# Keys of the last four groups turned by transfer from DRAM, a shorter warm-up, and two late scalings moved to VectorE

## The chip, the cores and the metric

The kernel runs on one core of a Trainium2 chip. The metric is the device time of one execution in microseconds (us). The engines of a core run side by side, each through its own list in order: TensorE (PE, its weight loads PEld), VectorE (DVE), ScalarE (ACT), GpSimd (POOL) and SyncE (SP), which here only issues transfers. They meet in semaphores. All numbers are fp32.

## What is computed

Two cross-attention layers over 128 batch items of 64 tokens (width 128). The first attends with the layer-normed tokens to two key sources (`a` and `v`) of 64 rows of width 64 each, then adds a dense layer with a residual. The second attends to the first source alone.

```
q = _ln(x1, g1, b1) @ Wq + bq;  k = _ln(x2, g2, b2) @ Wk + bk;  v = _ln(x2, g2, b2) @ Wv + bv
attn = softmax(einsum('bqe,bke->bqk', q, k) * scale);  ctx = attn @ v;  cma = ctx @ Wo + bo
output = cma_a(x, ctx_512) + cma_v(x, fside) + x
x = _ln(output, ln_g, ln_b) @ fc_W + fc_b + output
Q, K, V = x @ Wq + bq, ctx_512 @ Wk + bk, ctx_512 @ Wv + bv
out = x + softmax(Q K^T * scale) V @ Wo + bo
```

## The kernel before

Weights are folded once at the start (`fold_*` on PE, `copy_*` on ACT and DVE), so that Wq and Wk become one matrix `m0`. The rest is 16 groups of 8 batch items, all in tiles of 128 partitions x 512. One group passes on PE through: `t0` (queries times m0), `cfT` (keys transposed), `s0` (scores), `prob0T`, `mix0`, `out0`, `resN`, `dense`, `x1T`, then the second layer `t1`, `s1`, `prob1T`, `mix1`, `out1`. Between two of these steps another engine empties the PSUM bank: ACT copies and exponentials (`softmax0`, `softmax1`), four ACT scalings per group in `gain` behind `dense`, DVE statistics, maxima, sums and residuals, POOL the products that need no PSUM: `scale_cf` and `shift_cf` (layer norm of the keys), `scale_xt` (layer norm of queries that came already transposed), `probs0` and `probs1` (division by the softmax sum).

The order is written out by hand, engine by engine, as a list of calls; each call waits on semaphores for its inputs and for the buffer that it overwrites. A call that waits holds up all that stands behind it on its engine.

Three places matter here.

- **The ramp.** PE begins with `keep_busy`, multiplications of a constant (`ident` by `ones`) whose result nobody reads: 13, later 3, 1 and 1, eighteen in all. One such call is two matmul records in the trace.
- **The keys.** A group's keys come as `cf_sb` (key rows on partitions). DVE takes their statistics, ACT makes the reciprocal deviation, POOL `scale_cf` makes `cfv_sb` (also the values of `mix0`) and `shift_cf` makes `cfk_sb`, PE `cfT` transposes it with four 128x128 multiplications and ACT `copy_cfT` brings it to `cfT_sb`, which `s0` reads.
- **The spread of the scalings.** For groups 4 to 15 the queries come transposed, so that a token's scaling must lie along the free axis on every partition. PE `turn_rows(b)` transposes the 40 rows of scalings of a batch (two groups; batches 7 and 8 are groups 12, 13 and 14, 15), ACT `copy_rowsT` copies them, SP `store_rows` writes 20 KB to DRAM, SP `spread_x` reads it back to all 128 partitions (512 KB), POOL `scale_xt` multiplies. The code for the same with keys (`load_kt`, `spread_k`, `spread_s`, `scale_kt`, `shift_kt`) is there but not used, since `KEY_BATCHES` is empty.

Outputs leave through three slots of `out_sb` (`final` on DVE, `store` on SP).

Of the kernel before, what the change touches and what calls it, by code (L numbers as in the profile page):

```python
# [8 lines left out]
ALU = mybir.AluOpType  # L9
# [19 lines left out]
KEY_BATCHES = []  # L29
# [5 lines left out]
GAIN_ON_DVE = []  # L35
# [31 lines left out]
def attention_kernel(nc, x, xt, cf, kt, ct, wq, wk, wv, w128, wt, cols128, rows_dram, out):  # L67
    with ExitStack() as ctx:
# [3 lines left out]
        def sem(name):  # L72
# [76 lines left out]
        rsum1 = sb("rsum1", [P, GROUPS, PAIRS])  # L149
# [57 lines left out]
        exp1_bias_done, exp1_done, rsum1_done, prob1_done, final_done = (  # L207
            sem(s) for s in ("exp1_bias_done", "exp1_done", "rsum1_done", "prob1_done", "final_done"))
# [110 lines left out]
        def _(sp):  # L319
# [108 lines left out]
            load_x(11)
            store_rows(4)
            load_x(12)  # L430
            load_ct(4)
            load_x(13)
            load_xt(6)
            spread_x(4)
            load_ct(5)
            load_xt(7)
            load_cf(9)
            load_xt(8)
            load_xt(9)
            store_rows(5)  # L440
            load_x(14)
            load_cf(10)
            load_x(15)
            spread_x(5)
            load_cf(11)
            load_ct(6)
            store(0)
            store(1)
            load_xt(10)
            load_ct(7)  # L450
            load_ct(8)
            load_xt(11)
            load_xt(12)
            load_cf(12)
            store_rows(6)
            spread_x(6)
            load_cf(13)
            load_xt(13)
            store(2)
            load_ct(9)  # L460
# [12 lines left out]
            load_ct(13)
            spread_x(8)
            store(5)
            store(6)
            store(7)
            load_ct(14)
            load_ct(15)
# [12 lines left out]
        def _(pool):  # L492
# [89 lines left out]
            def probs1(g):  # L582
# [51 lines left out]
            scale_xt(8)
            probs1(3)
# [1477 lines left out]
```

## Time and profile before

| | |
|---|---|
| median of 3 runs | 154.44 us (153.74 to 155.4) |
| the profiled execution, its own time | 154.15 us |
| its span (first to last instruction) | 152.1 us |
| busy: PE, PEld, DVE | 144.1 (95%), 104.1 (68%), 119.7 (79%) us |
| busy: ACT, POOL | 117.0 (77%), 83.7 (55%) us |
| chain that ended last, by engine | PE 92%, ACT 3%, issue 2%, DVE 1% |
| moved by DMA | 23.40 MB, mean 154 GB/s |

The span is 2.05 us less than that execution's time; the rest lies outside the span. "Issue" is time in which an engine waited for nothing that the profile shows. A PE record's duration includes the drain of the array and overlaps the next, so what a block of PE work takes from the engine is read from its start to the next block's start.

### The profile page before, as it was taken

The numbers are of one execution on the slowest core, as the hardware profiler recorded it, in microseconds if no ns is written. First come the engines' busy times: TensorE is split into PE (matmuls) and PEld (weight loads), VectorE is DVE, ScalarE is ACT, GpSimd is POOL, SyncE is SP. The second block draws the span as 40 slices with busy tenths as digits, with TensorE's granted clock in tenths as the row PEclk, the third lists the DMA queues.
The fourth block names the chain that finished last, engine by engine and source line by source line (L and its number), as shares of the span: only waits on it lengthen the run. The fifth ranks groups of instructions, "written<-read, shape, count | busy, mean of one in ns | idle before, by whom it ended". The sixth has DMA issues, their size and how long they took to land.

```text
span 152.1 us, 6148 instructions
## 1 busy us (share of the span) xinstructions
PE 144.1 (95%) x2320; PEld 104.1 (68%) x2320; DVE 119.7 (79%) x351; ACT 117.0 (77%) x410; POOL 83.7 (55%) x112
## 2 busy tenths in 40 slices
PE   5999999799999999999999999999999999999771
PEld 5987767688566766656866767657874877766440
DVE  1557999968899979899889757988677799668733
ACT  3436778568989788967977999787996878796970
POOL 2566999679438861878177575595674141201220
PEclk9999999999999999999999999999999999999998
DMA  5995799570770608786445019707300402201215
GB/s 154 346 386 179 227 312 370 142 274 3 238 241 15 211 8 263 237 232 186 165 144 173 4 43 244 248 8 249 135 4 0 142 2 73 73 0 69 75 71 207
DMA packets 13449, 23.40 MB, mean 154 GB/s; under 512 B 1660, under 2 KB 4332, under 8 KB 13420
## 3 DMA queue, kind: packets, MB, share of 16 engines
q1 hardware_dynamic: 12988, 22.61, 45.6%
q8 instruction: 18, 0.29, 0.8%
q10 hardware_dynamic: 432, 0.41, 0.8%
q14 instruction: 11, 0.09, 0.2%
HBM read 18.69 MB, written 4.32 MB: 151 GB/s over the span
## 4 chain that ended last, share of the span: by engine, by line
PE 92%; ACT 3%; issue 2%; DVE 1%; POOL 0%; POOLq 0%; ACTq 0%
PE ps L1758 10%; PE ps L1740 10%; PE ps L1699 9%; PE ps L1773 6%; PE ps L1731 6%; PE ps L1709 6%; PE ps L1747 6%; PE ps L1766 5%; PE ps L1574 5%; PE ps L1808 5%; PE ps L1684 5%; PE ps L1719 5%; PE ps L1783 4%; PE ps L1800 3%; PE ps L1791 2%
## 5 line engine op out<-in xcount | busy, mean ns | idle before, releaser
L579 POOL TENSOR_TENSOR prob<-exp,rsum 128x512 f32<-128x512 f32 x16 | 16.7, 1044 | 23.6 <-DVE rsum L1231 23.4
L585 POOL TENSOR_TENSOR prob<-exp,rsum 128x256 f32<-128x256 f32 x16 | 9.8, 616 | 19.7 <-DVE rsum L1300 19.6
L539 POOL TENSOR_TENSOR cfv_sb<-cf_sb,rows 128x512 f32<-128x512 f32 x16 | 17.0, 1061 | 5.8 <-PE ps L1731 3.5
L844 ACT ACTIVATE exp<-ps,exp_bias 128x64 f32<-128x64 f32 x64 | 19.3, 322 | 1.0 <-DVE exp_bias L1295 0.9
L825 ACT ACTIVATE gain_sb<-ps,res_rstd 128x128 f32<-128x128 f32 x64 | 18.3, 372 | 1.6 <-PE ps L1758 1.2
L547 POOL TENSOR_TENSOR cfk_sb<-cfv_sb,rows 128x512 f32<-128x512 f32 x16 | 17.0, 1060 | 1.1 <-POOL rows L532 0.2
L1758 PEld LDWEIGHTS ps<-wd,resT_sb 128*128 128x128 f32 x128 | 15.8, 191 | 2.3 <-issue 1.9
L1758 PE MATMUL ps<-wd,resT_sb 128*128 128x130 f32 x128 | 17.3, 278 | 0.0
L1699 PE MATMUL ps<-zT_sb,m 128*128 128x512 f32 x32 | 17.0, 617 | 0.0
L1740 PE MATMUL ps<-mix_sb,w 128*128 128x512 f32 x32 | 16.8, 608 | 0.0
L555 POOL TENSOR_TENSOR zT_sb<-xt_sb,x_spread 128x512 f32<-128x512 f32 x12 | 15.2, 1278 | 2.7 <-DMA x_spread<-rows_dram 2.4
L1241 DVE SCALAR_TENSOR_TENSOR resT_sb<-ps,out_bias,xt_sb 128x512 f32<-128x512 f32 x16 | 12.0, 748 | 4.6 <-PE ps L1740 4.4
L1186 DVE BATCH_NORM_STATS2 cf_stats<-cf_sb 128x6 f32<-128x128 f32 x64 | 13.8, 281 | 1.1 <-DMA cf_sb<-in_cf 1.1
L844 ACT ACTIVATION_READ_ACCUMULATOR exp<-ps,exp_bias 128x1 f32 x64 | 13.7, 214 | 0.0
L1278 DVE SCALAR_TENSOR_TENSOR x1T_sb<-ps,row_bias,resT_sb 128x512 f32<-128x512 f32 x16 | 11.9, 741 | 2.2 <-PE ps L1766 1.9
L1308 DVE TENSOR_TENSOR out_sb<-ps,x1T_sb 128x512 f32<-128x512 f32 x16 | 11.0, 687 | 3.3 <-PE ps L1808 3.1
L1247 DVE BATCH_NORM_STATS2 res_stats<-ps 128x6 f32<-128x256 f32 x32 | 12.0, 417 | 1.8 <-PE ps L1747 1.7
L1227 DVE TENSOR_REDUCE sum<-exp 128x8 f32<-128x512 f32 x16 | 10.8, 678 | 3.0 <-ACT exp L802 2.9
L815 ACT COPY mix_sb<-ps 128x512 f32<-128x512 f32 x16 | 9.5, 592 | 4.5 <-PE ps L1731 4.5
L1216 DVE TENSOR_REDUCE max<-ps 128x8 f32<-128x512 f32 x16 | 10.9, 680 | 2.3 <-PE ps L1709 2.3
L789 ACT ACTIVATE t_sb<-ps,m 128x512 f32<-128x512 f32 x16 | 11.0, 689 | 2.1 <-PE ps L1699 2.0
L1179 DVE BATCH_NORM_STATS2 x_stats<-x_sb 128x6 f32<-128x256 f32 x32 | 11.9, 414 | 0.0
(148 smaller groups left out, 342.5 us busy)
## 6 DMA issues: line engine op xcount, KB each, us to landing
x_sb<-in_x SPq DMA_DIRECT2D x16, 256.0 KB, 3.8
xt_sb<-in_xt SPq DMA_DIRECT2D x16, 256.0 KB, 3.9
out<-out_sb SPq DMA_DIRECT2D x16, 256.0 KB, 2.2
cf_sb<-in_cf SPq DMA_DIRECT2D x15, 256.0 KB, 3.3
x_spread<-rows_dram SPq DMA_DIRECT2D x6, 512.0 KB, 4.7
ct_sb<-in_ct SPq DMA_DIRECT2D x16, 128.0 KB, 4.0
w_sb<-in_w SPq DMA_DIRECT2D x1, 448.0 KB, 4.5
cf_sb<-in_cf ACTq DMA_DIRECT2D x1, 256.0 KB, 4.5
```

Of the source, the lines that this page charges most:

```text
L539: pool.tensor_tensor(cfv_sb[:, g % CFV_SLOTS, :, :, :], cf_sb[:, g % CF_SLOTS, :, :, :], wide_cf(cf_rstd, g), ALU.mult).then_inc(cfv_pool, 1)
L547: pool.tensor_tensor(cfk_sb[:, at % CFK_SLOTS, :, :, :], cfv_sb[:, g % CFV_SLOTS, :, :, :], wide_cf(cf_shift, g), ALU.add).then_inc(cfk_po ...
L555: pool.tensor_tensor(zT_sb[:, g % ZT_SLOTS, :], xt_sb[:, g % XT_SLOTS, :], x_spread[:, slot, half, :], ALU.mult).then_inc(zT_scaled, 1)
L579: pool.tensor_tensor(prob0[:, g % PROB0_SLOTS, :, :, :], exp0[:, g % EXP0_SLOTS, :, :, :], wide0(rsum0, g), ALU.mult).then_inc(prob0_done, 1)
L825: last = nc.scalar.mul(gain_sb[:, g % GAIN_SLOTS, p, :], ps[:, bank + p // 2, at:at + D], res_rstd[:, g, p // 2, p % 2:p % 2 + 1])
L844: last = nc.scalar.activation(exp1[:, g % EXP1_SLOTS, p, :], ps[:, bank + u, v * S:(v + 1) * S], ACT.Exp, bias=exp1_bias[:, g, p:p + 1], a ...
L1186: last = v.bn_stats(cf_stats[:, g, p, :, :].rearrange("p h k -> p (h k)"), cf_sb[:, g % CF_SLOTS, p, :, :].rearrange("p h c -> p c h"))
L1241: v.scalar_tensor_tensor(resT_sb[:, g % REST_SLOTS, :], ps[:, bank, :], out0_bias[:, 0:1], xt_sb[:, g % XT_SLOTS, :], ALU.add, ALU.add).th ...
L1247: last = v.bn_stats(res_stats[:, g, u, :, :].rearrange("p v k -> p (v k)"), ps[:, bank, 2 * u * P:2 * (u + 1) * P].rearrange("p (v d) -> p ...
L1699: mm(ps[:, bank, :], m0[:, 0:2 * C], zT_sb[:, g % ZT_SLOTS, :], start=True, stop=True).then_inc(t0_made, 1)
L1740: mm(ps[:, bank, :], w01[:, 0:D], mix0_sb[:, g % MIX0_SLOTS, :, :, :, :], start=True, stop=True).then_inc(out0_made, 1)
L1758: last = mm(ps[:, bank + p // 2, at:at + D + 2], resT_sb[:, g % REST_SLOTS, p * P:(p + 1) * P], wd[:, 0:D + 2], start=True, stop=True)
```

## The change

1. `KEY_BATCHES = [7, 8]`: for groups 12 to 15 the keys are loaded a second time, already transposed (`load_kt`, 256 KB each). Their scalings and shifts are spread by `spread_k` and `spread_s` (two transfers of 256 KB each, four per batch). POOL `scale_kt` multiplies and `shift_kt` adds, straight into `cfT_sb`. `shift_cf`, `cfT` and `copy_cfT` of these groups are gone; `scale_cf` stays for the values.
2. Ten `keep_busy` multiplications instead of eighteen: 8 at the start and two single ones later. The folds stand in another order (`fold_wv` first), and so do the first loads.
3. `GAIN_ON_DVE = [14, 15]`: one DVE multiplication of 128x512 from PSUM (`early_gain`) in place of four ACT scalings, for the last two groups.
4. `PROB1_ON_DVE = [15]`: `probs1(15)` is made by DVE (`late_probs1`) instead of POOL, with a semaphore of its own.
5. The order of calls and the PSUM banks are new on every engine, from the first call to the last.

```diff
-KEY_BATCHES = []
+KEY_BATCHES = [7, 8]
-GAIN_ON_DVE = []
+GAIN_ON_DVE = [14, 15]
+PROB1_ON_DVE = [15]
...
+            def late_probs1(g):
+                dve.wait_ge(rsum1_done, g + 1)
+                need(dve, prob1T_made, g - PROB1_SLOTS + 1)
+                v.tensor_tensor(prob1[:, g % PROB1_SLOTS, :, :], exp1[:, g % EXP1_SLOTS, :, :],
+                                wide1(rsum1, g), ALU.mult).then_inc(prob1_dve, 1)
...
-            keep_busy(13, 0)
-            fold_v(0)
-            fold_a(6)
-            keep_busy(3, 2)
+            keep_busy(8, 0)
+            fold_wv(0)
+            fold_v(1)
+            fold_a(3)
```

The loaded keys' code, which was there before:

```
def spread_k(b):
    ...
    for h in range(2):
        sp.dma_start(k_spread[HALF[h], ...], rows_dram[at, 8 + 16 * h:16 + 16 * h, :]....broadcast_to([C, 8 * P]))
def scale_kt(g):
    pool.tensor_tensor(blocks(ks_sb[...]), kt_sb[...], blocks(k_spread[:, slot, half, :]), ALU.mult)
def shift_kt(g):
    pool.tensor_tensor(cfT_sb[...], blocks(ks_sb[...]), blocks(s_spread[:, slot, half, :]), ALU.add)
```

**The order on PE at the start.** Before, the first eleven rows after the entry (`ones,ident` is `keep_busy`, `wq_sb` and `wk_sb` the folds of the query and key weights, `z_sb` is `zT(0)`, `cols_sb,w_sb` `fold_bias`, `wkT_a,wqT_a` the first row of `fold_m0`):

```order
L1574 MATMUL ps<-ones,ident 128x128 x13
L1577 MATMUL ps<-affine_v,wq_sb 128x129
L1578 MATMUL ps<-affine_v,wk_sb 128x64
L1577 MATMUL ps<-affine_a,wq_sb 128x129
L1578 MATMUL ps<-affine_a,wk_sb 128x64
L1574 MATMUL ps<-ones,ident 128x128 x3
L1677 MATMUL ps<-ident,z_sb 128x128 x4
L1625 MATMUL ps<-cols_sb,w_sb 128x1
L1626 MATMUL ps<-cols_sb,w_sb 128x1
L1574 MATMUL ps<-ones,ident 128x128
L1604 MATMUL ps<-wkT_a,wqT_a 128x64
```

And of the change, in the same place (`wt_sb,w_sb` is the second row of `fold_am`, `affine_a,wv_sb` is `fold_wv`):

```order
L1592 MATMUL ps<-ones,ident 128x128 x8
L1635 MATMUL ps<-affine_a,wv_sb 128x65
L1635 MATMUL ps<-affine_v,wv_sb 128x65
L1595 MATMUL ps<-affine_v,wq_sb 128x129
L1596 MATMUL ps<-affine_v,wk_sb 128x64
L1595 MATMUL ps<-affine_a,wq_sb 128x129
L1596 MATMUL ps<-affine_a,wk_sb 128x64
L1643 MATMUL ps<-cols_sb,w_sb 128x1
L1644 MATMUL ps<-cols_sb,w_sb 128x1
L1664 MATMUL ps<-cols_sb,w_sb 128x1
L1665 MATMUL ps<-wt_sb,w_sb 128x64
L1622 MATMUL ps<-wkT_a,wqT_a 128x64
```

`zT(0)` now stands behind `fold_m0`, and `fold_wv` and `fold_am` ahead of it; four `keep_busy` between the folds are gone.

**The order on POOL in the last third.** Before, from `probs0(12)` on (`exp,rsum 128x512` is `probs0`, 128x256 `probs1`, `xt_sb,x_spread` is `scale_xt(14)` and `(15)`, `cfk_sb` is `shift_cf`):

```order
L579 TENSOR_TENSOR prob<-exp,rsum 128x512
L555 TENSOR_TENSOR zT_sb<-xt_sb,x_spread 128x512 x2
L585 TENSOR_TENSOR prob<-exp,rsum 128x256
L539 TENSOR_TENSOR cfv_sb<-cf_sb,rows 128x512
L579 TENSOR_TENSOR prob<-exp,rsum 128x512
L547 TENSOR_TENSOR cfk_sb<-cfv_sb,rows 128x512
L579 TENSOR_TENSOR prob<-exp,rsum 128x512
L585 TENSOR_TENSOR prob<-exp,rsum 128x256
```

And of the change, again from `probs0(12)` on (`ks_sb<-kt_sb,k_spread` is `scale_kt`, `cfT_sb<-ks_sb,s_spread` is `shift_kt`):

```order
L591 TENSOR_TENSOR prob<-exp,rsum 128x512
L567 TENSOR_TENSOR zT_sb<-xt_sb,x_spread 128x512 x2
L576 TENSOR_TENSOR ks_sb<-kt_sb,k_spread 128x512
L585 TENSOR_TENSOR cfT_sb<-ks_sb,s_spread 128x512
L576 TENSOR_TENSOR ks_sb<-kt_sb,k_spread 128x512
L597 TENSOR_TENSOR prob<-exp,rsum 128x256
L591 TENSOR_TENSOR prob<-exp,rsum 128x512
L585 TENSOR_TENSOR cfT_sb<-ks_sb,s_spread 128x512
L591 TENSOR_TENSOR prob<-exp,rsum 128x512
L597 TENSOR_TENSOR prob<-exp,rsum 128x256
```

Three key operations stand between `scale_xt(15)` and `probs1(9)` (the first row of 128x256), where none stood.

**The order on SP around the rows of batch 7.** Before (`rows_dram<-rowsT` is `store_rows(7)`, then `load_cf(14)`, `load_ct(10)`, `spread_x(7)`, `load_ct(11)`, `load_cf(15)`):

```order
L346 DMA rows_dram<-rowsT 40x128
L332 DMA cf_sb<-in_cf 128x512
L341 DMA ct_sb<-in_ct 128x256
L353 DMA x_spread<-rows_dram 128x1024
L341 DMA ct_sb<-in_ct 128x256
L332 DMA cf_sb<-in_cf 128x512
```

And of the change (`out<-out_sb` is `store(3)`, later `store(4)`; `cf_sb<-in_cf` is `load_cf(14)`, later `load_cf(15)`; the first `ct_sb` is `load_ct(12)`):

```order
L350 DMA rows_dram<-rowsT 40x128
L395 DMA out<-out_sb 128x512
L336 DMA cf_sb<-in_cf 128x512
L345 DMA ct_sb<-in_ct 128x256
L357 DMA x_spread<-rows_dram 128x1024
L367 DMA k_spread<-rows_dram 64x1024 x2
L395 DMA out<-out_sb 128x512
L336 DMA cf_sb<-in_cf 128x512
L377 DMA s_spread<-rows_dram 64x1024 x2
```

Two transfers for the scalings of the keys stand right behind `spread_x(7)`, and two for their shifts behind `store(4)` and `load_cf(15)`, which waits for `mix1(6)`.

## Rows read from the trace of the kernel before

**Rows 1.** The page: the chain that ended last, share of the span by engine.

```profile
PE 92%; ACT 3%; issue 2%; DVE 1%; POOL 0%; POOLq 0%; ACTq 0%
```

**Rows 2.** Stretches: us; PE, PEld, DVE, ACT, POOL busy; granted clock; DMA share; GB/s.

```profile
16.00:20.00 4.00, 4.00 (x52) 3.06 (x54) 3.97 (x15) 2.85 (x9) 3.91 (x7) 1.00 0.74 244
...
110.00:120.00 10.00, 10.00 (x179) 6.83 (x179) 7.77 (x20) 8.34 (x29) 5.27 (x6) 1.00 0.19 55
```

**Rows 3.** Timeline of the start: start us, us, engine line, idle before.

```profile
1.53 5.92 PE L1574 MATMUL ps<-ones,ident 128*128 128x128 f32 x26 [1.53 <-POOL ident L497]
1.64 0.55 SPq L378 DMA_DIRECT2D wk_sb<-in_wk  x1
...
7.24 0.54 PE L1577 MATMUL ps<-affine_v,wq_sb 128*128 128x129 f32 x2
...
8.85 0.94 PE L1574 MATMUL ps<-ones,ident 128*128 128x128 f32 x6
...
10.72 0.33 PE L1604 MATMUL ps<-wkT_a,wqT_a 128*128 128x64 f32 x2
...
12.13 1.12 PE L1699 MATMUL ps<-zT_sb,m 128*128 128x512 f32 x2
12.24 0.29 DVE L1149 COPY wvT<-ps 128x128 f32<-128x128 f32 x1 [1.29 <-PE ps L1617]
```

**Rows 4.** DMA issues: KB each, median us from issue to landing.

```profile
x_spread<-rows_dram SPq DMA_DIRECT2D x6, 512.0 KB, 4.7
...
wk_sb<-in_wk SPq DMA_DIRECT2D x1, 64.0 KB, 4.2
```

**Rows 5.** Timeline of PE, two of the 16 key transposes and what follows each.

```profile
85.51 0.60 PE L1684 MATMUL ps<-ident,cfk_sb 128*128 128x128 f32 x4
85.95 0.61 PE L1747 MATMUL ps<-ident,resT_sb 128*128 128x128 f32 x4
86.39 0.27 PE L1692 MATMUL ps<-ident,rows 128*40 128x128 f32 x1
...
119.33 0.60 PE L1684 MATMUL ps<-ident,cfk_sb 128*128 128x128 f32 x4
119.86 0.65 PE L1773 MATMUL ps<-x1T_sb,wd 128*64 128x256 f32 x4
```

**Rows 6.** Groups on POOL by line: busy, mean ns of one, idle before.

```profile
L547 POOL TENSOR_TENSOR cfk_sb<-cfv_sb,rows 128x512 f32<-128x512 f32 x16 | 17.0, 1060 | 1.1 <-POOL rows L532 0.2
...
L555 POOL TENSOR_TENSOR zT_sb<-xt_sb,x_spread 128x512 f32<-128x512 f32 x12 | 15.2, 1278 | 2.7 <-DMA x_spread<-rows_dram 2.4
```

**Rows 7.** Timeline of SP, POOL and PE: spread_x(7), scale_xt(12), t0(12), s0(12).

```profile
90.63 0.37 SPq L353 DMA_DIRECT2D x_spread<-rows_dram  x1
...
96.71 2.52 POOL L555 TENSOR_TENSOR zT_sb<-xt_sb,x_spread 128x512 f32<-128x512 f32 x2 [2.41 <-DMA x_spread<-rows_dram]
...
98.05 1.12 PE L1699 MATMUL ps<-zT_sb,m 128*128 128x512 f32 x2
...
102.83 0.64 PE L1709 MATMUL ps<-cfT_sb,t_sb 64*64 64x64 f32 x32
```

**Rows 8.** Timeline of the end: from dense(15) to the last probabilities.

```profile
137.40 1.06 PE L1758 MATMUL ps<-wd,resT_sb 128*128 128x130 f32 x8
...
138.58 1.15 ACT L825 ACTIVATE gain_sb<-ps,res_rstd 128x128 f32<-128x128 f32 x4
...
140.52 0.75 DVE L1278 SCALAR_TENSOR_TENSOR x1T_sb<-ps,row_bias,resT_sb 128x512 f32<-128x512 f32 x1
...
142.65 0.46 PE L1783 MATMUL ps<-ct_sb,t_sb 64*64 64x64 f32 x16 [0.28 <-ACT t_sb L834]
...
145.62 0.61 POOL L585 TENSOR_TENSOR prob<-exp,rsum 128x256 f32<-128x256 f32 x1 [0.70 <-DVE rsum L1300]
...
146.31 0.44 PE L1791 MATMUL ps<-ident,prob 128*128 128x128 f32 x2
```

**Rows 9.** A group on DVE, the nearest to the operations it gains.

```profile
L1222 DVE TENSOR_TENSOR diff<-ps,max 128x512 f32<-128x512 f32 x16 | 10.9, 684 | 0.3
```

More of the change, by code:

```diff
@@ L410, in _ @@
             load_xt(0)
+            load_kt(12)
             load_x(6)
@@ L428, in _ @@
+            load_kt(13)
             load_x(11)
             store_rows(4)
+            load_xt(8)
+            load_ct(3)
+            spread_x(4)
+            load_ct(4)
+            load_ct(5)
+            load_xt(9)
             load_x(12)
-            load_ct(4)
+            load_cf(9)
+            load_xt(10)
+            store_rows(5)
+            load_cf(10)
             load_x(13)
[L433 to L437, printed above, removed]
@@ L438, in _ @@
-            load_xt(8)
-            load_xt(9)
-            store_rows(5)
-            load_x(14)
-            load_cf(10)
-            load_x(15)
[L444 to L447, printed above, removed]
-            store(1)
[L449 to L455, printed above, removed]
+            load_xt(11)
+            load_x(14)
+            spread_x(5)
@@ L456, in _ @@
+            load_ct(6)
+            load_cf(11)
+            store(0)
+            load_kt(14)
+            load_xt(12)
+            load_ct(7)
+            load_x(15)
+            load_ct(8)
+            load_cf(12)
+            load_xt(13)
+            store_rows(6)
+            load_cf(13)
+            load_ct(9)
+            load_xt(14)
+            store(1)
+            store(2)
             spread_x(6)
[L457 to L460, printed above, removed]
+            load_ct(10)
@@ L472, in _ @@
             load_xt(15)
-            load_ct(13)
             spread_x(8)
-            store(5)
+            spread_k(8)
+            spread_s(8)
+            load_ct(15)
             store(6)
             store(7)
-            load_ct(14)
-            load_ct(15)
             store(8)
@@ L667, in _ @@
             scale_xt(15)
+            scale_kt(14)
+            shift_kt(14)
+            scale_kt(15)
             probs1(9)
-            scale_cf(15)
             probs0(13)
-            shift_cf(15)
+            shift_kt(15)
             probs0(14)
             probs1(10)
+            scale_cf(15)
             probs0(15)
@@ L1954, in _ @@
-            prob1T(6, 0, (prob1T_copied, 6))
-            mix1(5, 2)
-            s0(10, 4)
+            keep_busy(8, 0)
+            fold_wv(0)
+            fold_v(1)
+            fold_a(3)
+            fold_bias(7)
+            fold_am(5)
+            fold_m0(4)
+            zT(0, 6)
+            fold_w(0)
+            fold_bq1(1)
+            t0(0, 7)
+            cfT(0, 2)
+            fold_t1b(1)
+            zT(1, 7, (t0_copied, 1))
+            fold_fca(2, (cfT_copied, 1))
+            s0(0, 3)
```

1283 lines of the change are left out of this document (637 added, 646 removed).

## The prediction

> **What bounds the kernel now.** I read the chain of waits first, then the table of stretches, then the timelines of the ends. Of the chain that ended last 92% is PE [rows 1], and between 20 and 142 us the PE timeline stands almost without a gap: in the stretch from 110 to 120 PE is busy 10.00 of 10.00 us while POOL is busy 5.27 and ACT 8.34 [rows 2]. So in the middle only less PE work, or a wait that becomes longer than PE's work in hand, moves the end. Before that lies a ramp in which PE looks busy but partly does nothing useful: the first thirteen `keep_busy` (26 records) run from 1.53 to 7.24 [rows 3]. DVE is the full engine behind it, busy 3.97 of 4.00 us from 16 to 20 [rows 2]. Behind 142 us PE has run out of work and a serial chain remains: `s1(15)` at 142.65, softmax, `probs1(15)` on POOL at 145.62, its transpose at 146.31, and from there to 152.1 [rows 8].
>
> **Part 1, four key transposes less on PE.** A `cfT` block takes from its start to the next block's start 0.44 us (85.51 to 85.95) or 0.53 us (119.33 to 119.86) [rows 5]. Four of them are 1.8 to 2.1 us on the engine that bounds; I take **-1.9 us**. ACT loses four copies, which no wait of PE rests on.
>
> **Part 2, the same keys on POOL.** Four `shift_cf` of 1.06 us go [rows 6]. Eight products of two full 128x512 tiles come. The nearest row is `scale_xt`, the same form with a spread tile as second input: 1.28 us, or 2.52 for two in a row, 1.26 each [rows 6, 7]. The bounds for one are 1.06, the form with a small second input, and 1.28; I take 1.26, since the operands are those of `scale_xt`. POOL then has 8 x 1.26 - 4 x 1.06 = 5.8 us more, all in the last third. POOL was half idle there [rows 2], but only in sum; what counts is whether each product is ready when PE asks. I set both engines against each other from T, the start of `turn_rows(7)` (86.39 before [rows 5]).
>
> - *Start.* Before, `spread_x(7)` was issued at 90.63, T + 4.2, POOL waited 2.41 us for it and began `scale_xt(12)` at 96.71, T + 10.3; `t0(12)` began at 98.05, T + 11.7 [rows 7]. SP's queue still has `load_cf(14)` (behind `mix1(5)`) ahead of the spread, and that block stands five blocks behind `turn_rows(7)`, so the spread is issued at about T + 4 again. In the new order 24 blocks stand between `turn_rows(7)` and `t0(12)` where there were 23, with more long ones among them; by each kind's usual start-to-start time they sum to 12.0 us against 10.9. `t0(12)` is asked for at T + 12.0 or later and is ready at T + 11.6: no wait, with 0.4 us in hand.
> - *The run.* From `scale_xt(12)` to `shift_kt(12)` POOL has, in order, four tile products of this form with `shift_kt(12)` last (5.0), `probs0(10)`, `probs0(11)` and `scale_cf(13)` (about 1.0 each), `probs1(7)` and `shifts(8)` (0.6 and 0.5): 9.1 us, which ends at T + 19.4. The blocks up to `s0(12)` sum to 19.1 us by the same times. But these times are near the shortest; before, the same count gave 15.5 for T to `s0(12)`, and the trace has 16.4 (102.83) [rows 5, 7], 6% more. So PE asks at T + 19.1 to 20.3, POOL is ready at T + 19.4.
> - *The peak.* Between `probs0(12)` and `probs1(9)` POOL now has five tile products in a row, 6.3 us. Continuing the sum, `shift_kt(14)` ends at T + 29.8 against `s0(14)` at T + 29.7 to 31.4, `probs1(9)` at T + 31.6 against its transpose at T + 31.5 to 33.4, and `shift_kt(15)` at T + 33.9 against `s0(15)` at T + 35.2 to 37.4.
>
> The two engines run level for 25 us, with -0.3 to +2 us in hand at each meeting. Each time POOL is late, PE waits once and is in step again. I take **+0.6 us** for it in all; the bounds are 0 and 3 (if each product were met at the lower end and the spreads landed 2 us later, below). If the cover is gone, each tile product costs PE its whole 1.26 us.
>
> **Part 3, the spreads.** Batch 7 and 8 each issue `spread_k` and `spread_s`, four transfers of 256 KB, so eight issues of about 0.4 us on SP and 2 MB, and four `load_kt` of 256 KB. SP has nothing urgent behind them but `store` and `load_ct`. A 512 KB spread lands after 4.7 us [rows 4]; `spread_k(7)` follows `spread_x(7)` directly and is needed 3.4 us later on POOL (behind two scalings and `probs0(10)`), `spread_s(7)` waits in the queue for `mix1(6)`, about T + 9, lands near T + 15 and is needed at T + 18.2. Nothing for these, but it is the cover that is thinnest after POOL's.
>
> **Part 4, the ramp.** Eight `keep_busy` go. Five of the first thirteen at 0.44 each ((7.24 - 1.53) / 13) and three of the others at 0.22 (0.66 for three before `zT(0)`): 2.9 us is the most that can come back. The folds cannot start before their weights are there: `wk_sb` was issued at 1.64 and takes 4.2 us [rows 3, 4]; in the new order it stands one place later, about 2.2, so it lands at 6.4. `fold_v`, at 7.24 before, can start 0.8 us earlier. `fold_m0` began at 10.72 [rows 3], now it waits only for two copies and `fold_am`: about 8.8. Then `zT(0)` stands behind it and `t0(0)` behind the copy of that: 0.85 + 0.45 + about 1.1, so near 11.2 where it was 12.13. That is 0.9 us, and three folds that used to come later (`fold_am`, `fold_w`, `fold_bq1`, some 1.6 us) are done by then. But behind it DVE is full, and it gains only its own idle time: it stood 1.29 us before `copy_wv` for `fold_wv` [rows 3], which now comes first. I take **-1.3 us**; the bounds are 0 (the statistics are late because their loads are) and -2.9.
>
> **Part 5, the end.** `probs1(15)`: on POOL it took 0.61 us and from its start to the transpose 0.69 [rows 8]. On DVE, 684 ns for 128x512 [rows 9] makes 0.34 for half the columns, and the hop from DVE to POOL goes: **-0.3 us**, bounds 0 and -0.5. `gain(15)`: ACT took 1.15 us [rows 8], DVE about 0.69 [rows 9], 0.46 less; but in DVE's own list `x1(15)` now stands behind that product, `max_scores1(13)`, three small operations and `final(11)`, about 1.8 us, so `x1(15)` starts 0.7 + 1.8 + 0.1 behind the end of `dense(15)`. Before it was 140.52 - 138.46 = 2.1 [rows 8]. I count **+0.3 us**, bounds -0.5 and +0.8: what ACT gives up, DVE pays.
>
> **The sum** against the profiled execution: 152.1 - 1.9 + 0.6 - 1.3 - 0.3 + 0.3 = 149.5 us of span. With the 2.05 us outside the span 151.55; that execution's 154.15 is 0.3 under the median of 154.44, so the runs should centre at **151.8 us**, 1.7% less.
>
> TensorE's clock speaks against part 4. The first thirteen `keep_busy` run at 0.44 us each, the three at 8.85 at 0.22 [rows 3]: the lower level, 1.2 GHz, until about 7 us and the upper, 2.4 GHz, after, with the engine at work without pause before the rise; the granted clock column does not show it (1.00 in every stretch of rows 2). With eight, PE stops near 5 us and waits for weights. The Trainium skill ("TensorE: Matmul & The Clock Gate", Part 1: The HAM clock gate) says that the throttled state is the default and that sustained activity releases it, so a pause could keep the array slow; the rise behind steady work agrees with rows 3, and a fall behind a pause no row here shows. If the array stays at the lower level until `t0(0)`, each record of the folds takes up to twice its time, as 0.44 stands to 0.22: about 2 us more at most, 153.8 in all; this is part of the third rival.
>
> **The rivals.**
> - *As summed* (chance 0.52): -1% to -2.8%, 150.1 to 152.9.
> - *More comes back* (0.16): the whole 2.9 us of the ramp and no wait on POOL: 151.8 - 1.6 - 0.6 = 149.6. For it: three folds are out of the way early. Against it: DVE's 3.97 of 4.00.
> - *Little is left* (0.20): the ramp brings nothing, because the slow clock or late loads take it back, and POOL costs 1.5 instead of 0.6: 151.8 + 1.3 + 0.9 = 154.0. For it: the pause at 5 us, and a full DVE. A version in which DMA eats the transposes' gain ends in the same place.
> - *POOL becomes the bound* (0.12), the other side: a spread of batch 7 or 8 lands later than the 0.4 us in hand allows, because with 2 MB more the queues run behind each other. `scale_xt(12)` then holds up `probs0(10)`, `probs1(7)`, `probs0(11)`, and PE, which had 0.4 us in hand, waits for each. It decides when the spreads land 3.5 us later than 4.7 to 6: 3.2 us of wait cancel the gain, and 2 us more give 157. For it: POOL's level race. Against it: DMA was busy only 0.19 of its time from 110 to 120 [rows 2].
>
> That a part does nothing is in the third case. The measurement can tell about 1%, 1.5 us, from no change. Faster by over 1% (under 152.9): 0.68; within 1%: 0.20; slower: 0.12. The range from 149.4 to 154.6 leaves out the better half of the second case's spread and most of the fourth.
>
> **What would show it.** In the new trace: no transpose of `cfk_sb` beyond twelve; `t0(0)` near 11.2; the first folds' records as short as before (0.54 for the first pair) if the clock holds; `scale_kt` near 1.26 us; at `s0(12)`, `s0(14)` and `probs1(9)` waits of PE for POOL under 0.3 us each; POOL without a long idle time between T + 10 and T + 34; from `dense(15)` to the end about as long as before. Waits of POOL for a spread beyond 2.4 us, or gaps of PE that sum to over 2 us between 90 and 130, would make the prediction wrong on the slow side; `t0(0)` before 10.5 on the fast side.

## The result and the profile after

The changed kernel is slower: 158.4 us median (156.98 to 161.16, 4 runs) against 154.09 us for the kernel before (153.29 to 155.4, 4 runs). The ratio is 1.024, 95% interval 1.013 to 1.036. The prediction was 151.8 us. The profiled execution took 156.98 us with a span of 155.2, 3.1 more than before. It is the fastest of the four, so the trace explains 3.1 us and not the whole 4.3 between the medians. The medians are of all runs, but the ratios leave out runs over 1.5% above the fastest of their kernel, such as the one of 161.16 us here, three of e1's four with its profiled one, and e7's profiled one. The first rows are lines of the page: the span, the busy tenths of PE, PE's granted clock and DMA in 40 slices of 3.9 us, what DMA moved, and the chain that ended last, by engine.

```profile
span 155.2 us, 6094 instructions
PE   6799999999999999999999999889987999999771
PEclk9955699999999999999999999999999999999999
DMA  4994847599693229396067269916992120002215
DMA packets 14665, 26.54 MB, mean 171 GB/s; under 512 B 1852, under 2 KB 4524, under 8 KB 14636
PE 75%; DMA 12%; ACT 4%; issue 3%; DVE 2%; POOL 1%; SPq 1%; POOLq 0%
```

PE fell from 92% of the chain [rows 1] to 75%, and DMA entered it with 12%. Two places stand out: the clock's "556" in slices 3 to 5 (8 to 20 us), and PE's 8, 8 from 97 to 105 us and 8, 7 from 113 to 120, where it had no gap before. The table of stretches gives their size (stretch, length, busy time of PE, PEld, DVE, ACT, POOL, granted clock, DMA share, GB/s):

```profile
8.00:12.00 4.00, 4.00 (x25) 3.81 (x24) 3.80 (x16) 1.48 (x6) 2.96 (x5) 0.51 1.06 386
12.00:16.00 4.00, 4.00 (x16) 2.76 (x16) 1.15 (x5) 1.10 (x4) 2.60 (x5) 0.50 0.39 139
16.00:20.00 4.00, 4.00 (x51) 3.36 (x50) 3.00 (x13) 3.00 (x11) 1.37 (x4) 0.71 0.79 256
100.00:110.00 10.00, 9.50 (x157) 6.88 (x159) 7.82 (x24) 7.68 (x31) 8.60 (x11) 1.00 0.53 153
110.00:120.00 10.00, 8.66 (x182) 5.72 (x178) 6.87 (x17) 6.46 (x22) 7.03 (x6) 1.00 0.70 181
```

Before, DVE was busy 3.97 of 4.00 us from 16 to 20, and PE 10.00 of 10.00 from 110 to 120 at a DMA share of 0.19 [rows 2]. From 12 to 16 PE now reads as fully busy and makes 16 records, where the kernel before makes 51:

```profile
8.00:12.00 4.00, 4.00 (x38) 3.67 (x36) 2.24 (x10) 1.75 (x6) 2.25 (x4) 1.00 1.06 385
12.00:16.00 4.00, 3.91 (x51) 2.85 (x51) 3.76 (x15) 2.98 (x11) 3.12 (x5) 1.00 0.57 174
```

**Where the 3.1 us come from.** I gave each PE block its usual start-to-start time and summed, for both kernels, what had not started yet at a given time. The new kernel has 1.8 us less in all (four `cfT`). At 30 us both have the same left (107.5 and 107.7), so the ramp has already cost what the transposes give, 1.8 us. The lag is still zero at 95 us, 1.3 at 110, 2.9 at 120 and 3.0 at 130. Blocks of one kind do not always take the same time, so these sums are good to some tenths of a us. From `dense(15)` to the end of the span it is 14.85 us against 14.7. So: ramp +1.8, transposes -1.8, middle +3.0, end +0.1.

**The ramp.** PE's first fold, with the idle time before it and what ended it:

```profile
5.91 0.43 PE L1635 MATMUL ps<-affine_a,wv_sb 64*128 64x65 f32 x2 [0.83 <-DMA wv_sb<-in_wv]
```

Eight `keep_busy` end at 5.08, the weights are there at 5.9, and from 8 to 16 us the granted clock is 0.50, which is 1.2 GHz. `t0(0)` starts at 14.71, where it was 12.13.

**The middle.** What PE waited for from 85 to 130 us (line, releaser, total, times, longest), and then the instructions behind it, with `turn_rows(7)` at 84.74 as T:

```profile
PE ps L1749 <- issue: 1.1, 1, 1.1
PE ps L1737 <- POOL prob L591: 0.5, 1, 0.5
PE ps L1710 <- POOL rows L544: 0.4, 1, 0.4
PE ps L1717 <- POOL zT_sb L567: 0.2, 1, 0.2
```

```profile
90.49 0.38 SPq L357 DMA_DIRECT2D x_spread<-rows_dram  x1
...
94.55 0.34 SPq L336 DMA_DIRECT2D cf_sb<-in_cf  x1
...
106.38 0.33 SPq L357 DMA_DIRECT2D x_spread<-rows_dram  x1
...
100.53 0.89 DVE L1195 BATCH_NORM_STATS2 cf_stats<-cf_sb 128x6 f32<-128x128 f32 x4 [1.57 <-DMA cf_sb<-in_cf]
...
102.10 0.24 POOL L541 TENSOR_TENSOR cf_sr<-cf_stats,rows 128x16 f32<-128x16 f32 x1 [1.25 <-ACT rows L772]
...
113.12 2.50 POOL L567 TENSOR_TENSOR zT_sb<-xt_sb,x_spread 128x512 f32<-128x512 f32 x2 [1.36 <-DMA x_spread<-rows_dram]
```

These waits sum to 2.3 of the 3.0 us of lag; where the other 0.7 goes is not shown. `load_cf(15)` goes out at 94.55 between the new spreads, T + 9.8, and lands 6.0 us later. In the kernel before it took as long (6.1), but went out at T + 5.1. DVE waits 1.57 us for it, then ACT's logs, then POOL's `shifts(8)`. `turn_rows(8)` comes at 102.79, T + 18.05 (T + 14.5 before), `spread_x(8)` is issued at 106.38, and `scale_xt(14)` waits for it until 113.12.

### The profile page after: what moved, and what is told of

It is laid out like the page before. It is cut to its first block, busy times and chain, and to the rows that moved or that the text cites. A ratio compares the mean times of both kernels' runs of the same rounds, so it can differ in the third digit from the quotient of the medians.

```text
span 155.2 us, 6094 instructions
## 1 busy us (share of the span) xinstructions
PE 144.8 (93%) x2288; PEld 103.3 (67%) x2288; DVE 123.3 (79%) x354; ACT 112.5 (73%) x398; POOL 89.0 (57%) x115
## 4 chain that ended last, share of the span: by engine, by line
PE 75%; DMA 12%; ACT 4%; issue 3%; DVE 2%; POOL 1%; SPq 1%; POOLq 0%
PE ps L1717 9%; PE ps L1776 9%; PE ps L1758 7%; PE ps L1791 5%; PE ps L1749 5%; PE ps L1727 5%; PE ps L1737 4%; PE ps L1765 4%; PE ps L1784 4%; DMA cf_sb<-in_cf 4%; PE ps L1702 4%; DMA x_spread<-rows_dram 3%; PE ps L1826 3%; PE ps L1818 3%; DMA wv_sb<-in_wv 3%
## 5 line engine op out<-in xcount | busy, mean ns | idle before, releaser
L597 POOL TENSOR_TENSOR prob<-exp,rsum 128x256 f32<-128x256 f32 x15 | 9.2, 612 | 19.7 <-DVE rsum L1309 19.6
L1717 PE MATMUL ps<-zT_sb,m 128*128 128x512 f32 x32 | 18.0, 646 | 0.2 <-POOL zT_sb L567 0.2
L840 ACT ACTIVATE gain_sb<-ps,res_rstd 128x128 f32<-128x128 f32 x56 | 16.0, 375 | 2.2 <-PE ps L1776 1.8
L823 ACT COPY prob0T_sb<-ps 128x512 f32<-128x512 f32 x16 | 9.5, 595 | 5.0 <-PE ps L1737 4.7
L559 POOL TENSOR_TENSOR cfk_sb<-cfv_sb,rows 128x512 f32<-128x512 f32 x12 | 12.7, 1058 | 0.5 <-POOL rows L544 0.2
L1749 PEld LDWEIGHTS ps<-prob0T_sb,cfv_sb 64*64 64x64 f32 x512 | 9.3, 134 | 5.3 <-issue 2.6
```

The source lines that it names most:

```text
L559: pool.tensor_tensor(cfk_sb[:, at % CFK_SLOTS, :, :, :], cfv_sb[:, g % CFV_SLOTS, :, :, :], wide_cf(cf_shift, g), ALU.add).then_inc(cfk_po ...
L840: last = nc.scalar.mul(gain_sb[:, g % GAIN_SLOTS, p, :], ps[:, bank + p // 2, at:at + D], res_rstd[:, g, p // 2, p % 2:p % 2 + 1])
L1717: mm(ps[:, bank, :], m0[:, 0:2 * C], zT_sb[:, g % ZT_SLOTS, :], start=True, stop=True).then_inc(t0_made, 1)
L1749: last = mm(ps[HALF[h], bank + v, at:at + S], cfv_sb[HALF[v], g % CFV_SLOTS, 2 * u + b, h, :], prob0T_sb[HALF[v], g % PROB0T_SLOTS, h, u, ...
```

## The experiments

Two questions: what slowed the ramp (the pause that eight constants leave, or the new order), and what slowed the middle. For the middle the rivals were POOL's 5.8 us more (theory 3), the late `cf(15)` alone (5), the traffic of the new transfers (6), and the later place of `turn_rows(8)` in the new order (7). The kernel before ran beside each of them: 154.02 us median beside e1 to e4, 154.08 beside e5 to e8, 153.6 beside e9 to e11. Ratios are to that. A saving given between two runs is the difference of their ratios.

### e1 and e2: how many constants, in either kernel

```diff
-            keep_busy(8, 0)
+            keep_busy(13, 0)
```

> The changed kernel with keep_busy(13, 0) in place of keep_busy(8, 0) at the start. In the changed kernel PE stands idle for 0.83 us before the first fold at 5.91, and the granted clock is 0.50 to 0.51 from 8 to 16 us; t0(0) starts at 14.71 where it stood at 12.13 before. Theory 1 (the pause let the clock fall and this costs about 2 us): with thirteen constants the granted clock is 1.0 through the ramp, t0(0) starts near 11.5 to 12.5, and the time is about 2 us under the changed kernel's. Theory 2 (the clock fall would come anyway, or the ramp is late because of its new order of loads, folds and statistics): t0(0) stays at 14 to 15 us and the time stays within 0.7 us of the changed kernel's.

```diff
-            keep_busy(13, 0)
+            keep_busy(8, 0)
```

> The kernel before with keep_busy(8, 0) in place of keep_busy(13, 0) at the start, nothing else. Theory 1 (shortening this stretch alone makes PE pause and drops the clock): PE stops near 5 us and waits for the weights until about 5.9 or later, the granted clock falls to 0.5 within the next 10 us, t0(0) comes at 14 us or later instead of 12.13, and the time rises by about 2 us. Theory 2 (the ramp's loss comes from the changed kernel's new order): the granted clock stays at 1.0, and the time is the same or up to 0.8 us less, as the first fold can start 0.8 us earlier.

**e2: 157.25 us, ratio 1.020 (1.013 to 1.028).** One number in the old kernel costs 3.2 us. PE's first fold behind the pause, and two stretches:

```profile
6.46 0.46 PE L1577 MATMUL ps<-affine_v,wq_sb 128*128 128x129 f32 x2 [1.53 <-DMA wk_sb<-in_wk]
```

```profile
8.00:12.00 4.00, 4.00 (x19) 3.88 (x19) 2.06 (x9) 1.38 (x5) 2.50 (x4) 0.50 1.06 384
12.00:16.00 4.00, 4.00 (x18) 2.62 (x18) 1.74 (x10) 0.97 (x5) 1.73 (x2) 0.50 0.30 109
```

`t0(0)` comes at 14.15 and `t0(1)` at 19.43, 3.7 us late. In the old order this is the pause's doing, since the kernel before, which differs in nothing else, reads 1.00 in these stretches. The Trainium skill ("TensorE: Matmul & The Clock Gate", Part 1: The HAM clock gate) makes the throttled state the default that activity releases. The trace of e2 agrees: PE had worked from 1.52 to 4.93, stood for 1.53, and was at 0.50 from 8 us on.

One thing stays open. Of e2's four runs two have a mean granted clock of 0.97 (156.46 and 156.94 us, the profiled one), and two of 1.00 (157.56 and 157.72), which were no faster; the changed kernel too has a run of 158.42 us at 1.00. The column also reads 1.00 for the first constants, which run at the lower level [rows 3]. So in those runs PE may have stayed low from the start, but no trace of them was kept. What the shorter start costs is shown; that all of it is the fall at 8 us is shown for the profiled runs only.

**e1: 156.87 us in its fastest run** (the others 160.8 to 163.4), level with the changed kernel's fastest, 156.98. Theory 1 in its simple form falls: there is no pause, and the clock falls all the same.

```profile
8.00:12.00 4.00, 4.00 (x32) 3.46 (x31) 2.25 (x9) 1.69 (x7) 1.41 (x4) 0.87 1.05 386
12.00:16.00 4.00, 4.00 (x17) 2.88 (x16) 2.35 (x12) 1.28 (x5) 3.48 (x6) 0.50 0.41 145
```

From 7.4 to 11.5 us this kernel runs nothing but small folds, the last of them of one column. `t0(0)` starts at 15.05. PE is busy 4.00 of 4.00 us in both rows, so this fall follows no idle time. All four runs have a mean granted clock of 0.95 to 0.98.

### e7 and e10: the constants between the folds

```diff
-            keep_busy(8, 0)
+            keep_busy(13, 0)
...
             fold_a(3)
+            keep_busy(3, 6)
             fold_bias(7)
+            keep_busy(2, 6)
             fold_am(5)
             fold_m0(4)
+            keep_busy(2, 6)
```

> The changed kernel with keep_busy(13) at the start and keep_busy(3), (2) and (2) between the folds, as many constants as the kernel before had in its ramp. In e1, with thirteen at the start and none between the folds, PE never stood still and yet the granted clock was 0.87 from 8 to 12 us and 0.50 from 12 to 20. Theory 1b (not the pause alone but the stretch of small folds, which does little work in the array, lets the clock fall; the constants between them held it): granted clock 1.00 up to 30 us, t0(0) between 11.5 and 13.5 instead of 14.71, and 1.5 to 3 us less than the changed kernel. Rival (the clock falls for another reason, or the new order of the ramp is late by itself): the clock falls again near 11 us, or it holds and t0(1) still comes after 19 us.

```diff
-            keep_busy(3, 2)
             zT(0, 2)
             fold_bias(3)
-            keep_busy(1, 0, (wq_v_done, 1), (wk_v_done, 1))
-            fold_m0(0)
+            fold_m0(0, (wq_v_done, 1), (wk_v_done, 1))
```

> The kernel before without keep_busy(3, 2) and keep_busy(1, 0) between the folds; the thirteen at the start stay. PE has no pause before the first fold, as in e1. Theory 1b (the constants between the small folds hold the clock): the granted clock falls to 0.5 behind about 11 us and the time rises by 2 to 3 us, as in e2. Rival (only the pause at 5 us matters, and e1 fell for another reason): granted clock 1.00 and the time the same or 0.5 us less.

**e7: 156.32 us, ratio 1.014 (1.005 to 1.022).** Against the changed kernel's 1.024 that is 1.6 us less, and the intervals overlap. Against e6 below, which has the changed kernel's ramp and ran beside e7, it is 2.6 us less, and they do not. The granted clock is 1.00 throughout the ramp, as expected (0.99 to 1.00 as the mean of each of the four runs):

```profile
8.00:12.00 4.00, 4.00 (x37) 3.66 (x37) 2.91 (x13) 1.47 (x6) 2.06 (x4) 1.00 1.05 390
12.00:16.00 4.00, 4.00 (x30) 3.13 (x30) 2.51 (x11) 2.00 (x7) 2.90 (x6) 1.00 0.38 136
```

`t0(0)` at 14.24 missed its 11.5 to 13.5, since the added constants stand in its way: seven between the folds, 1.8 us, where the kernel before has four. But `t0(1)` is at 18.54 instead of 20.30.

**e10: 152.13 us, ratio 0.989 (0.984 to 0.994), faster than both kernels.** Theory 1b expected it slower, and is wrong for the old order:

```profile
8.00:12.00 4.00, 3.96 (x33) 3.17 (x32) 3.61 (x19) 2.93 (x10) 3.83 (x6) 1.00 1.06 387
```

```profile
9.90 1.12 PE L1699 MATMUL ps<-zT_sb,m 128*128 128x512 f32 x2
```

The clock stays at 2.4 GHz without the inner constants, and `t0(0)` starts 2.2 us earlier. Only 1.1 of these are the constants left out. The rest is luck of this run: the clock rose earlier, the thirteen constants took 4.7 us instead of 5.9, and the first fold started at 6.08 instead of 7.24 [rows 3]. The ratio, over five runs, stands beside that. So the constants between folds are needed in the one order and are pure cost in the other. In e10 a transpose, `zT(0)`, stands among the folds and `t0(0)` follows at 9.90; in e1 the run of small folds goes on to 11.5. That this is the difference fits both, but no run tried it alone.

### e3: the key path in the old order

`KEY_BATCHES = [7, 8]` in the old kernel, with four `cfT`, `copy_cfT` and `shift_cf` out, and the new calls in by hand. On POOL:

```diff
             scale_xt(13)
+            scale_kt(12)
+            shift_kt(12)
             shifts(8)
```

> The kernel before with the keys of groups 12 to 15 turned from DRAM and scaled on POOL, put in by hand: four cfT, their copies and four shift_cf go, eight products of 1.27 us on POOL, four loads of keys and four spreads come; ramp, order of the other work and end stay as before. It has no other part of the change. Theory 3 (the new path itself costs more than it gives, because its products make POOL late for PE and its spreads delay other loads): 1 to 3 us slower than before, with PE waiting for POOL between 95 and 130 us. Theory 4 (the path gives 1.9 us of PE and takes back 0.6, and the changed kernel's loss of 3 us between 95 and 130 comes from how the new order places the late loads and copies): 0 to 1.3 us faster than before.

**161.95 us, ratio 1.048 (1.040 to 1.057)**, worse than either theory said. What PE waited for:

```profile
PE ps L1700 <- POOL rows L540: 5.0, 1, 5.0
```

`shift_kt(12)` waited 3.3 us for `s_spread`, and `shifts(8)`, which the whole next batch needs, stood behind it: my own placement, so this run prices one wrong position and not the path. The changed kernel's order has `shifts(8)` ahead.

### e4, e6, e5: which resource it is

```diff
-X_SLOTS, XT_SLOTS, CF_SLOTS, KT_SLOTS, CT_SLOTS, SPREAD_SLOTS = 4, 8, 9, 3, 6, 2
+X_SLOTS, XT_SLOTS, CF_SLOTS, KT_SLOTS, CT_SLOTS, SPREAD_SLOTS = 4, 8, 10, 3, 6, 2
...
             load_cf(14)
+            load_cf(15)
             load_ct(12)
...
-            load_cf(15)
```

> The changed kernel with ten slots for cf_sb in place of nine, and load_cf(15) issued right behind load_cf(14), so that it waits for no mix1(6) and lies ahead of spread_x(7) and spread_k(7) in SP's queue. In the changed kernel that load is issued at 94.55 and lands at 100.5, and through statistics, logs, shifts(8), turn_rows(8) and store_rows(8) spread_x(8) is issued only at 106.38 and scale_xt(14) starts at 113.12. Theory 5 (this chain is what makes PE idle between 100 and 120): turn_rows(8) starts at T + 16 or earlier instead of T + 18.05, PE is busy 9.8 of 10 us in both stretches, and the time is 1.5 to 3 us less. Theory 3 (POOL's 5.8 us more are the cause): POOL is late at s0(12) and s0(14) all the same, and the time stays within 0.7 us of the changed kernel's.

**158.69 us, ratio 1.028 (1.021 to 1.036): no gain.** DVE no longer waits for `cf(15)`, but its statistics stand so late in DVE's list that they begin at 101.52 anyway; `turn_rows(8)` comes at T + 17.2. `spread_x(8)` is issued at 107.78, and now its own landing is the wait:

```profile
115.80 2.49 POOL L567 TENSOR_TENSOR zT_sb<-xt_sb,x_spread 128x512 f32<-128x512 f32 x2 [2.34 <-DMA x_spread<-rows_dram]
```

Theory 5, that this one load is the cause, falls.

```diff
-                pool.tensor_tensor(blocks(ks_sb[:, at % KS_SLOTS, :]), kt_sb[:, at % KT_SLOTS, :, :, :, :],
-                                   blocks(k_spread[:, slot, half, :]), ALU.mult).then_inc(ks_done, 1)
+                pool.tensor_tensor(blocks(ks_sb[:, at % KS_SLOTS, :])[:, 0:1], kt_sb[:, at % KT_SLOTS, 0:1, :, :, :],
+                                   blocks(k_spread[:, slot, half, :])[:, 0:1], ALU.mult).then_inc(ks_done, 1)
```

(and `shift_kt` in the same way)

> The changed kernel in which scale_kt and shift_kt work on half of their tile's columns (the keys' other half stays what an earlier group left there: that part of the result is left out), so that POOL has about 8 x 0.6 = 5 us less to do; all transfers and the order stay. Theory 3 (POOL's 5.8 us more hold up PE): the time falls by 2 to 3 us. Theories 6 and 7 (transfers, or order): POOL only waits longer for its spreads and rows, turn_rows(8) stays 17 to 18 us behind turn_rows(7), and the time stays within 0.8 us of the changed kernel's.

**158.36 us, ratio 1.030 (1.023 to 1.038): the changed kernel's time.** The eight products took 0.73 us each instead of 1.27, 4.3 us less on POOL, and PE's waits are as before:

```profile
L585 POOL TENSOR_TENSOR cfT_sb<-ks_sb,s_spread 128x256 f32<-128x256 f32 x4 | 2.9, 730 | 1.7 <-issue 1.7
L576 POOL TENSOR_TENSOR ks_sb<-kt_sb,k_spread 128x256 f32<-128x256 f32 x4 | 2.9, 730 | 0.0
```

```profile
PE ps L1749 <- issue: 1.6, 1, 1.6
PE ps L1737 <- POOL prob L591: 1.1, 1, 1.1
PE ps L1710 <- POOL rows L544: 0.4, 1, 0.4
```

Lines that name POOL as the releaser do not mean that POOL is short of time: it stood idle for its inputs. Theory 3 falls.

```diff
             spread_x(5)
+            spread_k(7)
+            spread_s(7)
+            spread_k(8)
+            spread_s(8)
```

> The changed kernel with the eight transfers of spread_k and spread_s issued right behind spread_x(5), from batch 5's rows, so that they move the same 2 MB some 30 us earlier and no product waits for them (the scalings of groups 12 to 15 then multiply the keys by another batch's rows: that part of the result is left out). POOL does the same eight products in the same order. Theory 6 (the transfers late in the kernel hold up cf(15), the rows and spread_x(8), and so PE between 95 and 130 us): load_cf(15) lands in about 4 us instead of 5.96, store_rows(8) in under 2 instead of 2.98, scale_xt(14) starts at least 2 us earlier against turn_rows(7), and the time is 1.5 to 3 us under the changed kernel's 158.4. Theory 3 (POOL's own work): no more than 0.7 us less. Theory 7 (the new order of the engines places turn_rows(8) late, 17 to 18 us behind turn_rows(7) instead of 14.5): about 1 us less at most.

**166.22 us, ratio 1.068 (1.056 to 1.079).** Theory 6 said 1.5 to 3 us less; by the ratios it is 6.7 us more. The transfers do their harm where they go:

```profile
60.00:70.00 10.00, 7.36 (x111) 5.48 (x103) 9.20 (x28) 6.75 (x23) 4.46 (x5) 0.99 0.87 241
70.00:80.00 10.00, 7.41 (x118) 4.35 (x118) 1.62 (x8) 3.03 (x10) 2.73 (x3) 0.84 1.02 297
```

DMA is full from 70 to 80, DVE has work for 1.62 of 10 us, and from 80 to 90 the clock falls to 0.66 as well. The stretch was already used for `x` and `cf` loads. The run speaks for traffic as the cause, against my wish for a cheap place to put it.

### e9 and e11: traffic alone, and traffic away

```diff
             spread_x(7)
+            more_spreads(7, 8)
...
             load_cf(15)
+            more_spreads(7, 16)
...
             spread_x(8)
+            more_spreads(8, 8)
+            more_spreads(8, 16)
```

(`more_spreads` issues what `spread_k` and `spread_s` issue; four `more_kt` likewise)

> The kernel before plus the transfers of the key path alone: four loads of keys and eight spreads of 256 KB each, at the places in SP's queue that they have in e3, into tiles that nothing reads. PE, DVE, ACT and POOL do exactly what they do in the kernel before. In e6 POOL had 5 us less to do and the time did not move, so POOL's work is out; what is left is traffic or order. Theory 6 (traffic): spread_x(8) and the loads land later, PE stands still at its 1693rd matmul record, where it stands still for 1.0 to 2.9 us in e1, e3, e7 and e8, whatever block is there, and the time rises by 1.5 to 3 us. Theory 7 (order): within 0.7 us of the kernel before, no stop at record 1693.

**157.78 us, ratio 1.025 (1.019 to 1.030).** No compute engine has any more to do, and it costs 3.8 us. Every PE record up to 97 us starts within 0.1 us of its old time. Then:

```profile
97.67 2.49 POOL L576 TENSOR_TENSOR zT_sb<-xt_sb,x_spread 128x512 f32<-128x512 f32 x2 [3.43 <-DMA x_spread<-rows_dram]
...
98.99 1.12 PE L1720 MATMUL ps<-zT_sb,m 128*128 128x512 f32 x2 [1.04 <-POOL zT_sb L576]
...
102.09 0.88 DVE L1207 BATCH_NORM_STATS2 cf_stats<-cf_sb 128x6 f32<-128x128 f32 x4 [3.62 <-DMA cf_sb<-in_cf]
...
103.66 0.24 POOL L550 TENSOR_TENSOR cf_sr<-cf_stats,rows 128x16 f32<-128x16 f32 x1 [2.48 <-ACT rows L778]
...
104.31 0.27 PE L1713 MATMUL ps<-ident,rows 128*40 128x128 f32 x1 [2.44 <-POOL rows L553]
```

This is the changed kernel's chain with longer waits. From issue to landing `spread_x(7)` takes 7.3 us instead of 6.0 with the key spreads beside it, `load_cf(15)` 8.9 instead of 6.1, and statistics, logs, shifts and `turn_rows(8)` follow; PE's two waits are 3.5 us. The key spreads themselves took 7.5 and 9.1 us (median) from issue to landing. The stop at record 1693 that I expected did not come.

```diff
-                                   blocks(k_spread[:, slot, half, :]), ALU.mult).then_inc(ks_done, 1)
+                                   blocks(x_spread[:, spread_at(g)[0], half, :]), ALU.mult).then_inc(ks_done, 1)
...
-            spread_k(7)
...
-            spread_s(7)
```

(on top of e7; `shift_kt` and batch 8 likewise)

> e7 (the changed kernel with its ramp's clock held) without the eight transfers of spread_k and spread_s: scale_kt and shift_kt take x_spread as second operand, a tile of the same shape that is there earlier (the scalings of the keys of groups 12 to 15 are left out of the result). POOL's products, their number and all orders are those of e7; 2 of the 3.1 MB more are gone. Theory 6 (traffic): the stop at record 1693 goes or falls under 0.5 us, scale_xt(14) starts 1 to 2 us earlier against turn_rows(7), and the time is 2 to 3 us under e7's 156.3. Theory 7 (order): turn_rows(8) still stands 17 to 18 us behind turn_rows(7), PE's waits for prob0(10) and rows stay, and the time stays within 0.8 us of e7's.

**152.38 us, ratio 0.994 (0.990 to 0.998)**: 1.9% or 3.0 us under e7 (1.6 to 4.4), as theory 6 expected, with POOL's work and all orders as in e7. `load_cf(15)` lands after 2.9 us where e7 has 5.7, `spread_x(7)` after 5.2 for 6.6, `spread_x(8)` after 4.7 for 6.9. Of PE's waits between 85 and 130 us one of 0.2 us is left, and PE is busy 10.00 of 10.00 again:

```profile
110.00:120.00 10.00, 10.00 (x214) 6.59 (x208) 8.34 (x21) 8.50 (x34) 7.84 (x8) 1.00 0.15 54
```

`turn_rows(8)` still stands at T + 16.5, so the later place in the new order is real and costs nothing by itself. Theory 7 falls, theory 6 stands. Of e7's 3.4 us of waits in its profile, 2.4 are a stop with "issue" as the releaser, which is gone here too; the last section is about these.

### e8: both mended by hand

`e7` plus ten slots for `cf_sb`, batch 7's spreads right behind `store_rows(7)`, batch 8's right behind `store_rows(8)`, and `stats_cf(15)`, `cf_logs(8)`, `shifts(8)` and `turn_rows(8)` moved forward.

```diff
             store_rows(7)
+            load_xt(15)
+            spread_x(7)
             load_cf(14)
+            load_cf(15)
+            spread_k(7)
+            spread_s(7)
```

> The changed kernel with the constants of e7, and with the second batch's rows brought forward: ten slots for cf_sb, load_cf(15) and the spreads of batch 7 issued right behind store_rows(7), statistics of cf(15), its logs, shifts(8) and turn_rows(8) four to ten instructions earlier in the lists of DVE, ACT, POOL and PE, and the spreads of batch 8 right behind store_rows(8). If both theories hold (clock in the ramp, late rows and spreads in the middle): turn_rows(8) starts 15 us behind turn_rows(7), PE is busy at least 9.8 of 10 us from 100 to 120, and the time is 150 to 152.5 us, under that of the kernel before. If POOL's own work is the cause in the middle: 154 to 156. If neither is right: as the changed kernel, 157 to 158.

**156.61 us, ratio 1.018 (1.011 to 1.025), not told apart from e7**, where 150 to 152.5 was expected. The waits for POOL nearly vanish, and PE stops elsewhere, for nothing that the profile shows:

```profile
99.26 0.63 PE L1749 MATMUL ps<-prob0T_sb,cfv_sb 64*64 64x64 f32 x27 [1.84 <-issue]
...
113.53 0.45 PE L1727 MATMUL ps<-cfT_sb,t_sb 64*64 64x64 f32 x13 [1.04 <-issue]
```

My reordering of the queue did not win back what the traffic costs.

## Why the prediction was wrong

Its sum for the span was 149.5; it was 155.2. Of the 5.7 us the ramp is 3.1 and the middle 2.4.

- **Part 1, the transposes, -1.9: right.** 48 records of `cfT` instead of 64, 1.8 us less on PE.
- **Part 2, POOL's run, +0.6: right in the sizes, wrong in what ruled them.** The products took 1.27 us for the 1.26 taken. Between their inputs POOL kept up, and e6 shows that its work costs nothing. But the times from T were missed, and both signs that the prediction had named for the slow side came: POOL stood 3.35 us before `scale_xt(12)`, until `spread_x(7)` had landed at 95.4, and PE's gaps sum to 2.3 us (`spread_x(7)` issued at T + 5.75 for T + 4, `s0(12)` T + 22.0 for T + 19.1 to 20.3). They rest on loads and spreads.
- **Part 3, the spreads, "Nothing for these": the wrong step.** I asked only whether the new transfers would land in time for their own readers, and all but one did: `shift_kt(14)` stood 0.90 us until `s_spread(8)` had landed at 117.6, and PE did not wait for it. I did not ask what they do to transfers already there. In e9 `load_cf(15)` took 8.9 us for 6.1, and `spread_x(7)` held POOL for 3.43 us where it was 2.41 [rows 7]. Their price is 3.0 us in the new order (e11 against e7) and, with the key loads, 3.8 in the old (e9). In the changed kernel's own profile the slower landing is plain only for `spread_x(8)`, 6.6 us for 5.0: `spread_x(7)` (4.9 for 6.0) and `load_cf(15)` (6.0 for 6.1) took no longer there than before, but went out later. My argument against it was a DMA share of 0.19 from 110 to 120 [rows 2]. In the stretch in which batch 7's spreads run it was 0.68 in the kernel before (the row below), and 0.87 in the changed one:

```profile
90.00:100.00 10.00, 9.97 (x197) 7.24 (x194) 8.97 (x27) 7.99 (x28) 6.09 (x6) 1.00 0.68 202
```

  The fourth rival had the mechanism ("a spread lands later"), its place and the waits, at a chance of 0.12; its condition of 3.5 us later was too strict. Its name, POOL as the bound, does not fit e6, and by its own terms its last figure should be 156.4, not 157: the sum already holds 0.6 of the 3.2 us of wait.
- **Part 4, the ramp, -1.3: wrong in sign, +1.8.** The paragraph on the clock named what happened and priced it at 2 us at most; I gave it a part of one rival. e2 shows 3.2 us for the shorter start alone. (The three constants before `zT(0)` take 0.77 us, from 8.85 to 9.62 [rows 3], not 0.66; this changes nothing.) Some time was to be had: e10 gets 1.1% by leaving out constants where PE keeps working. In the new order of folds the clock falls even without a pause (e1), and the old trace holds no row of such an order. So in the changed kernel the pause is not shown to be the one cause of the fall.
- **Part 5, the end, 0: right.** `probs1(15)` took 0.42 us on DVE where I had 0.34, and 14.85 us for 14.7 from `dense(15)` on.

## What to carry to other kernels

A transfer that is not urgent itself still delays those that are: look at the DMA share of the very stretch in which it runs, and find what lands there with little in hand. Cut warm-up work only as far as PE does not have to wait behind it, compare several runs, and read the granted clock of the next stretches, not PE's busy share. When a wait names a busy engine, halve that engine's work in an experiment before believing it; here it was idle.

## What the runs showed of the hardware that was not expected

**Stops of PE at fixed instruction numbers.** In kernels of quite different order PE stood still with "issue" as the releaser, often in the middle of a block. Counting matmul records from the start up to the stop (the count in the first brackets) gives:

```profile
0.00:117.00 117.00, 113.38 (x1693) 82.85 (x1693) 94.52 (x278) 85.69 (x291) 75.52 (x101) 0.94 0.66 203
```

```profile
0.00:118.00 118.00, 109.71 (x1693) 79.58 (x1693) 92.51 (x280) 87.09 (x301) 77.49 (x102) 0.99 0.67 199
```

```profile
0.00:111.50 111.50, 108.03 (x1693) 79.23 (x1693) 93.59 (x277) 84.42 (x287) 74.98 (x100) 1.00 0.69 212
```

These are e1, e3 and e7 (stops of 2.85, 1.58 and 2.42 us); e8 stops at 1693 as well. e4 and e8 stop at 1446, e4 also at 582, the kernel before, e3 and e9 at 335 (1.01 us in the kernel before), and 1693 - 1446 = 582 - 335 = 247. The changed kernel and e6 stop one record earlier, at 1692. The page lists a DMA queue of kind "instruction" with 18 packets and 0.29 MB, 16 KB each. That PE's instructions arrive by that queue and come late when transfers crowd is my reading. The times of these packets in the traces speak for its first half: in each of the fourteen stops of this kind of 0.15 us or more in the thirteen traces PE goes on 1.3 to 1.7 us behind the end of such a packet. In e7 the 13th of them starts at 111.51 us, with a DMA share of 1.02 in the 4 us before, and PE stops at its 1693rd record until 114.09. In e11 the 13th starts earlier in PE's list, at record 1630, with a share of 0.62, and PE does not stop. The second half is not shown. Against traffic as the only condition: e9 has the same transfers and no stop at 1693. For it: in e11, with 2 MB less, the only stop is one of 0.21 us, at record 1941 (1693 + 248). What makes the packet late stays open. In the changed kernel's profile 1.1 of the middle's 2.3 us of waits are this; in how far they would be there without the late loads is open too.

**Clock falls in the middle of the kernel.** Around long stops the granted clock fell there too: 0.66 from 80 to 90 us in e5, with a wait of 4.1 us that ended at 81.5, and 0.83 from 110 to 120 in e7, with its stop of 2.42 us. e9's wait of 2.44 us had no fall behind it. Where the clock falls, a wait is paid twice.
